# Whole last batch with eight PSUM banks in turn, and the first four weight pieces passed in halves (one core)

## The reference, cut to what matters

```
cond = einsum(x, W) + b + 2 * (x @ lora_As[slot]) @ lora_Bs[slot]      # x: (8, 512, 2048)
logits = einsum(cond, route_w)                                          # 8 experts
wh = one_hot(argmax(logits)) * max(logits) * einsum(cond, A)            # rank 16 each
out = x + einsum(wh, Bw)                                                # back to 2048
```

## Time and profile before

| | us |
|---|---|
| median of 3 runs | 286.09 (285.75 to 286.72) |
| profiled execution | 285.52 |
| its span | 283.7 |
| TensorE busy | 278.7 (98%) |
| VectorE busy | 201.8 (71%) |
| ScalarE busy | 112.5 (40%) |

### The profile page before, as it was taken

The page is one execution under the profiler, slowest core; times in us unless marked ns, Lnnn a source line. Parts: engine busy times, 40 slices in busy tenths (PEclk is TensorE's granted clock), DMA queues, the critical chain, the costliest instruction groups (busy, mean ns, idle before and its releaser), DMA issues.

```text
span 283.7 us, 4398 instructions
## 1 busy us (share of the span) xinstructions
PE 278.7 (98%) x1699; PEld 225.3 (79%) x1699; DVE 201.8 (71%) x234; ACT 112.5 (40%) x166; POOL 15.0 (5%) x46
## 2 busy tenths in 40 slices
PE   8999999999999999999999999999999999999994
PEld 5999999997766885888588758857885887588994
DVE  0052200077598999699789969996998798699975
ACT  0001301196786532734274355427432742442300
POOL 7600030000000000000000000000000000000000
PEclk9999999999999999999999999999999999999999
DMA  7999999999991066849967993999399769636668
GB/s 241 404 407 395 399 413 412 373 398 417 418 419 70 39 259 234 358 151 405 400 231 258 425 386 136 373 393 395 137 379 409 267 211 398 281 148 249 267 237 285
DMA packets 19303, 88.52 MB, mean 312 GB/s; under 512 B 2378, under 2 KB 4818, under 8 KB 11474
## 3 DMA queue, kind: packets, MB, share of 16 engines
q1 hardware_dynamic: 16128, 85.15, 76.8%
q10 hardware_dynamic: 3154, 3.09, 3.3%
HBM read 54.60 MB, written 33.55 MB: 311 GB/s over the span
## 4 chain that ended last, share of the span: by engine, by line
PE 98%; DVE 0%; DVEq 0%; issue 0%
PE bank_out L693 16%; PE bank_h L770 11%; PE bank_h L771 10%; PE bank_h L772 10%; PE bank_out L730 10%; PE bank_out L732 10%; PE bank_out L731 10%; PE bank_e L755 10%; PE bank_e L693 1%; PE bank_l L706 1%; PE bank_l L693 1%; PE bank_h L693 1%; PE bank_r L693 1%; PE bank_h L699 1%; PE bank_r L790 1%; PE bank_h L783 1%
## 5 line engine op out<-in xcount | busy, mean ns | idle before, releaser
L433 ACT ACTIVATE x_hi<-x_ring 128x1024 fp32r<-128x1024 f32 (+1 forms) x72 | 68.9, 965 | 63.5 <-PE bank_h L772 63.0
L535 DVE TENSOR_TENSOR x_lo<-x_ring,x_hi 128x1024 fp32r<-128x1024 f32 (+1 forms) x72 | 78.8, 1103 | 9.3 <-ACT x_hi L433 8.7
L628 DVE TENSOR_TENSOR x_ring<-bank_out,x_ring 128x1024 f32<-128x1024 f32 (+1 forms) x71 | 78.5, 1107 | 1.7 <-PE bank_out L732 1.3
L770 PE MATMUL bank_h<-x_hi,m_hi 128*128 128x512 f32 (+1 forms) x144 | 53.5, 372 | 0.0
L771 PE MATMUL bank_h<-x_lo,m_hi 128*128 128x512 f32 (+1 forms) x144 | 52.7, 366 | 0.0
L772 PE MATMUL bank_h<-x_hi,m_lo 128*128 128x512 f32 (+1 forms) x144 | 52.6, 366 | 0.0
L730 PE MATMUL bank_out<-wh_hi,bw_hi 128*128 128x512 f32 (+1 forms) x143 | 52.5, 367 | 0.0
L731 PE MATMUL bank_out<-wh_lo,bw_hi 128*128 128x512 f32 (+1 forms) x143 | 52.4, 366 | 0.0
L732 PE MATMUL bank_out<-wh_hi,bw_lo 128*128 128x512 f32 (+1 forms) x143 | 52.4, 366 | 0.0
L770 PEld LDWEIGHTS bank_h<-x_hi,m_hi 128*128 128x128 f32 x144 | 27.1, 188 | 11.2 <-issue 5.9
L693 PE MATMUL bank_out<-pt,w_ring 128*128 128x136 f32 x288 | 34.5, 279 | 0.0
(11 more groups left out here) (96 smaller groups left out, 188.7 us busy)
## 6 DMA issues: line engine op xcount, KB each, us to landing
x_ring<-xT SPq DMA_DIRECT2D x32, 1024.0 KB, 7.8
outT<-x_ring SPq DMA_DIRECT2D x28, 1024.0 KB, 5.0
w_ring<-W SPq DMA_DIRECT2D x30, 512.0 KB, 10.8
outT<-x_ring SPq DMA_DIRECT2D x12, 256.0 KB, 2.7
x_ring<-loraB ACTq DMA_DIRECT2D x8, 128.0 KB, 10.2
la<-loraA ACTq DMA_DIRECT2D x8, 128.0 KB, 13.1
x_ring<-BwT SPq DMA_DIRECT2D x1, 1024.0 KB, 11.6
pt<-PT SPq DMA_DIRECT2D x3, 272.0 KB, 8.9
```

Source lines behind the costliest of these rows:

```text
L433: act.activation(out, in_, ACT.Copy).then_inc(done, 1)
L535: dve.tensor_tensor(out, a, b, ALU.subtract).then_inc(done, 1)
L628: dve.tensor_tensor(x, out_banks(u, j), x, ALU.add).then_inc(v_out, 1)
L770: mm(h, m_hi[:, c, :], hi, start=(c == 0), stop=False)
```

## The change

Two edits. At the start, the first four pieces of W are all cut in two halves of two row chunks each, and TensorE passes over the four pieces twice: the first halves of pieces 0 to 3, then the second halves. At the end, the last batch is one unit of 512 tokens as the others are. Its output steps use all eight banks in turn, as four buffers of two (`bank_e` and `bank_h` become the two halves of `bank_eh`, `bank_r` and `bank_l` those of `bank_rl`), three output steps of batch 6 are held back behind its main product, and its stores are 512 KB per pair of chunks and 256 KB for each of the last two chunks. x and the output of the last batch lie in HBM as those of the other batches do. The diff, cut to its core:

```diff
-        UNITS = [(b, 0, T) for b in range(NB - 1)] + [(NB - 1, t, T // 2) for t in (0, T // 2)]
-        HELD = [2] * (NU - 1) + [3]
+        HELD = [2] * (NB - 1) + [3]
...
+        def w_bank(blk):
+            return (*bank_out, bank_eh, bank_rl)[blk] if blk < OPEN else bank_out[blk % 2]
+        def out_bank(b, j):
+            if b < NB - 1:
+                return bank_out[j % 2]
+            return (bank_eh, *bank_out, bank_rl)[j % 4]
+        def store_last(eng, c0, c1):
+            j = c0 // 2
+            k = NPIECES - NQ + 2 * T * j // PIECE
+            at = T * c0 % PIECE
+            eng.wait_ge(v_out, NP2 * (NB - 1) + (j + 1 if c1 - c0 == 2 else c1 - j))
+            eng.dma_start(outT[k, :, at:at + (c1 - c0) * T], x_ring[:, k % XRING, at:at + (c1 - c0) * T]).then_inc(d_last, 16)
...
+            def load_open(h):
+                sp.dma_start(head_sb[:, h, :], head[h]).then_inc(d_head[h], 16)
+                for n in range(1, OPEN):
+                    blk, part = ORDER[n]
+                    o = slice(h * HO, (h + 1) * HO)
+                    sp.dma_start(w_ring[:, n, o, :], W[blk, part, :, o, :]).then_inc(d_w_half[n - 1] if h == 0 else d_w[n], 16)
...
-            for n in range(NWP):
-                load_w(n)
+            for h in range(NHEAD):
+                load_open(h)
+            for n in range(OPEN - 1, NWP):
+                if n >= OPEN:
+                    load_w(n)
...
-            for u in range(NB - 1, NU):
-                for j in range(NP2):
-                    if u < NU - 1 or j % 2 == 0:
-                        store_pair(sp, u, j)
-            store_single(sp, 1)
+            for j in range(0, NP2 - 1, 2):
+                store_last(sp, 2 * j, 2 * j + 2)
+            store_last(sp, C - 1, C)
...
+            def w_open(h):
+                for n in range(OPEN):
+                    if n == 0:
+                        pe.wait_ge(d_head[h], 16)
+                    elif h == 0:
+                        pe.wait_ge(d_w_half[n - 1], 16)
+                    else:
+                        pe.wait_ge(d_w[n], 16)
+                    last = w_rows(n, h * HO, (h + 1) * HO)
+                    if h == NHEAD - 1:
+                        last.then_inc(t_w, 1)
...
+            for h in range(NHEAD):
+                w_open(h)
+            for n in range(OPEN, BP_AT):
                 w_piece(n)
...
+                if b == 0 and j < 2:
+                    pe.wait_ge(v_m, NWB)
+                elif b < NB - 1:
+                    pe.wait_ge(v_out, NP2 * b + j - 1)
+                elif j == 0:
+                    pe.wait_ge(v_two, NB)
+                    pe.wait_ge(v_wh, NB)
+                elif j == 3:
+                    pe.wait_ge(v_w, NB)
+                    pe.wait_ge(v_ahead, NB)
                 else:
+                    pe.wait_ge(v_out, NP2 * b + j - (2 if j < 3 else 3))
```

More of the change, by code:

```diff
@@ L215, in loads_in_slot, with x_pair @@
             return n // WRING + (1 if n % WRING else 0)
[L217 to L223, removed]
         def x_landed(eng, k):
             eng.wait_ge(d_x[k % XRING], 16 * (k // XRING + 1))
[L229 to L251, removed]
+        def x_pair(b, j):
+            at = 2 * T * j % PIECE
+            return x_ring[:, (NQ * b + 2 * T * j // PIECE) % XRING, at:at + 2 * T].rearrange("p (c t) -> p c t", c=2)
         WARM_UP = 8
@@ L437, in m_block, with split_hi @@
                 act.wait_ge(t_w, DONE[n])
[L438 to L447, removed]
+                sums = w_bank(n)[:, :, 0:PN]
+                copy(m_hi[:, 2 * n:2 * n + 2, :], sums[:, :, E:PN], a_m)
+                for i in range(2):
+                    copy(ext[i][:, 2 * n:2 * n + 2, 0:E], sums[:, :, 0:E], a_m)
+            def split_hi(b, j):
+                g = NP2 * b + j
+                if b == 0 and j < SRING:
                     act.wait_ge(t_w, NWP - WRING + j + 1)
@@ L648, in _ @@
                     if j < SRING:
-                        if j >= 2 or not short(u):
-                            split_lo(u, SRING + j)
-                    elif u + 1 < NU:
-                        split_lo(u + 1, j - SRING)
-                    if u >= 1 and 1 <= j <= NP2 - HELD[u]:
-                        add_x(u - 1, j - 1)
-                if u >= 1:
-                    weigh(u)
-                    add_x(u - 1, NP2 - HELD[u])
-                weigh_lo(u)
-                if u >= 1:
-                    for j in range(NP2 - HELD[u] + 1, NP2):
-                        add_x(u - 1, j)
+                        split_lo(b, SRING + j)
+                    elif b + 1 < NB:
+                        split_lo(b + 1, j - SRING)
@@ L662, in _ @@
+                    if b >= 1 and 1 <= j <= NP2 - HELD[b]:
+                        add_x(b - 1, j - 1)
+                if b >= 1:
+                    weigh(b)
+                    add_x(b - 1, NP2 - HELD[b])
+                weigh_lo(b)
+                if b >= 1:
+                    for j in range(NP2 - HELD[b] + 1, NP2):
+                        add_x(b - 1, j)
             for j in range(NP2 - 1):
-                add_x(NU - 1, j)
+                add_x(NB - 1, j)
             for i in range(2):
-                x = x_pair(NU - 1, NP2 - 1)[:, i, :]
@@ L671, in _, with w_rows @@
             mm = pe.matmul
+            def w_rows(n, o0, o1):
+                blk, part = ORDER[n]
+                for i in range(2):
+                    bank = w_bank(blk)[:, i, 0:PN]
+                    for o in range(o0, o1):
+                        k = part * WO + o
+                        for p in range(NPT):
+                            if blk == 0 and i == 0 and k == PT_PARTS[p][0]:
+                                pe.wait_ge(d_pt[p], 16)
+                        last = mm(bank, w_chunk(n, o, i), pt_chunk(k), start=(k == 0), stop=(k == C - 1))
+                return last
+            def w_open(h):
[9 more added lines that the diff above has]
+                        last.then_inc(t_w, 1)
             def w_piece(n):
```

288 lines of the change are left out of this document (102 added, 186 removed).

## The result

| | us |
|---|---|
| before, median of 7 runs | 286.09 (285.49 to 286.77) |
| changed, median of 7 runs | 287.63 (287.18 to 288.02) |
| ratio | 1.0051, interval [1.0034, 1.0067] |
| changed, profiled execution | 287.64, span 285.8 |

The change makes the kernel slower, by 1.54 us. The forecast was 286.8; the time is 0.83 above it (0.3%) and lies in the range, but the loss is about twice the 0.7 us that was forecast.

What follows compares the result with a forecast made beforehand. The prediction took the last store bytes, behind full DMA engines, to end the kernel, not the last matmul. Opening +0.25 and stores +0.5 us on 286.09 gave 286.8 us, range 285.7 to 288.3.

Steps and rivals of the forecast that it cites:

- The last bytes end both kernels: End: the last store bytes, at about 282.4 us before and 282.9 changed, set the end, not the last matmul.
- TensorE 1.36 earlier: End: with the last batch whole, the last matmul starts at 278.09 us against 279.45, 1.36 us earlier.
- no wait for `wh_lo`: Batch 7's first output step: three held steps cover the operand, ready about 0.8 us early; otherwise 0.6 us waited.
- Stores +0.5: End: stores with 4 KB rows at 403 GB/s end at 282.9 us against 282.4; bounds 0.1 to 1.8 us.
- The opening +0.25: Opening: TensorE's early gain is lost and it is 0.25 us late at piece 28 of W; range -0.15 to +0.9.
- the rows' cost of 0.4 us: Opening: four DMAs with 2 KB rows in place of 4 KB delay the full DMA stream by 0.4 us.
- W28 lands at a fixed time: Phase 1: the full DMA stream lands piece 28 of W at 60.48 + 0.4 us, however early it is issued.
- rival 4: Opening: its gain comes through, -0.5 us, with +0.5 at the end: 286.1, no change; chance 0.22 shared with another rival.
- Rival 1: End: 4 KB row stores leave at 440 GB/s or more, so the end follows VectorE: 285.1 us; chance 0.09.
- Rival 3: Both ends: W halves at 283 GB/s, pairs at 354, +0.9 and +1.8 us: 288.8; chance 0.14 with its like.
- What was to be seen: Changed profile: slow 4 to 9 us windows, last matmul near 278.3, full DMA share 270 to 283, last store over 3 us.
- The wait at W28: Phase 1: the first weight load of W's piece 28 waits for its DMA near 60.7 to 61.2 us.

Runs made afterwards that it cites:

- e1: The changed kernel with the opening of the kernel before, so only the whole last batch is changed: 287.50 us, ratio 1.0049 to the kernel before.
- e4: The changed kernel without ScalarE's stores of steps 1, 3 and 5 of the last batch (1.57 MB not written): 285.72 us, ratio 0.9985.
- e6: The changed kernel with two output steps held back at the last batch in place of three: 287.71 us, ratio 1.0056.
- e7: The changed kernel with the last batch's output through the two old buffers in turn, not four: 286.63 us, ratio 1.0030.
- e9: The changed kernel less two needless TensorE waits before the last batch's first output step, one instruction less: 287.05 us, ratio 1.0039.
- e5: The changed kernel with 192 more instructions (fulfilled waits) on TensorE's queue: 286.44 us, ratio 1.0015.
- e10: The kernel before with 64 more TensorE instructions, fulfilled waits ahead of the first 8 `bank_e` matmuls of each batch: 287.07 us, ratio 1.0031.
- e2: The kernel before with only the new opening, the first four pieces of W passed in halves: 285.66 us, ratio 0.9984.
- e3: The changed kernel with 96 more instructions (fulfilled waits) on TensorE's queue: 286.62 us, ratio 1.0022.
- e8: The kernel before with the new opening and its last batch's stores joined in twos to 4 KB rows: 286.24 us, ratio 1.0013.

## Why the prediction was right or wrong

- **The last bytes end both kernels: right.** e1 carries the loss, e4 takes it away, e6 and e7 delay TensorE by 0.6 and 1.1 us and the median does not follow.
- **TensorE 1.36 earlier, no wait for `wh_lo` that counts: right.** The last matmul was foretold for 278.09 without the opening's shift; it starts at 278.82 with one of 0.63, and 0.1 of waits. VectorE: 279.6 foretold, 280.31 less 0.63 is 279.7.
- **Stores +0.5: right in mechanism and rate, but not the whole end.** 403 GB/s was taken for 4 KB rows, 398 to 401 measured in these windows and 404 in e9's. The bulk ends at about 283.4, and 282.9 was foretold before the opening's shift. Without the load the profiles say +0.4 to +0.8 (43.0 to 43.4 against 42.6) and the medians +0.5 to +1.1, within the bounds of 0.1 to 1.8.
- **The missing term: one load of instructions.** The chain "the bytes end, the kernel ends" took the sixteen engines as one. 16 KB on a single engine take about 1 us: in the changed kernel's window from 275 to 276 us they are 6.0% of sixteen engines, 0.96 us of one. A store alone fills all sixteen (share 1.01 from 256.5 to 259.0), so the last one lands with the engine that is behind. That engine ends 1.5 us behind the others, more than the load's own 0.96; where the rest comes from is not shown. The load is worth 1.0 us in the profiles. In medians it is 0.4 by the two increases over the kernel before (changed 1.54, e9 1.13), 0.8 against e5, and 1.15 in e10. The sum was 0.83 too low, and this is the term that it lacked. That it falls there is inferred from the program's length: it is shorter by 97 matmuls and as many weight loads (1602 against 1699), so the place in it at which the last of the 13 loads is due comes later in time. Before, it was 266.9, when the stores had slack. Nothing in the earlier trace rows shows it; only the packets by queue do.
- **The opening +0.25: wrong in sign, and its mechanism with it.** e2 gives -0.46, interval -0.86 to -0.09. Two steps failed: the rows' cost of 0.4 us, and that W28 lands at a fixed time however early TensorE is. With the halves it landed at 60.62 in the changed kernel, 60.55 in e2, 60.8 in e3, 60.1 in e4, e6 and e9, and 59.8 in e5, e7 and e8. With the old opening it was 60.48, and 60.2 in e1 and 60.6 in e10. So no delay by short rows can be seen in a spread of 1.0 us. The wait that e3 shows at 60.84 is one execution's. In e5's, where the full rate came early, piece 4 starts at 11.68, 0.55 us earlier than before. W28 has landed at 59.8, and TensorE takes it at 60.09, 0.56 earlier:

```profile
60.09 1.93 PEld L612 LDWEIGHTS bank_out<-head_sb,w_ring 128*128 128x128 f32 x16
```

The gain passed through, as rival 4 has it (-0.5 for the opening), and e2's median fits that. Why it does not in e2's own profiled execution (60.66, as before) stays open. So does why it does not appear with the new end (e1 287.50 and changed 287.63, of different rounds).
- **Luck in the number.** The opening was put 0.7 us too high by e2 (+0.25 against -0.46), and the end lacked a term of about 1.0. The two errors go against each other, and the forecast came within 0.3% with the opening's half of its mechanism wrong.
- **Rival 1 (stores keep up at 440): wrong**: from 275 to 280 us the stores of the changed end move 397 to 406 GB/s in every kernel that has them all. **Rival 3: wrong**, 401 is not 354, and W28 was not 0.9 late. The Trainium skill, DMA: Bandwidth & Descriptors, Specifications, with 512 B as the least transfer for line rate, agrees with W28's landings, which the 2 KB rows of the opening did not delay, and not with the stores: 354 GB/s with 2 KB rows, 401 with 4 KB, 419 with 8 KB. The size of one store grows with the row in all three, so these runs do not tell the two apart.
- **What was to be seen:** the windows from 4 to 9 us under 396 (266, 373), the last matmul near 278.3 plus the shift, and the last store over 3 us (5.0) came true, and the share from 270 to 283 nearly so (0.93 to 1.03). (The windows say little: from 6 to 9 us e1, with the old opening, moves 376 GB/s.) The wait at W28 is missing in the changed kernel's profile, which the prediction had named as a sign of being wrong. TensorE's late rise to the full rate hides it there, but the landings above say the same.

The best of these kernels is e2, the opening without the new end: 0.9984 of the kernel before.

## What to carry to other kernels

When a kernel ends in stores that fill the DMA engines, count engine by engine: a share of 0.06 behind the bulk is one engine that is late, and the list of packets by queue says what else was moved in that stretch. A kernel whose program grows or shrinks by a few instructions can move its instruction loads; before crediting or blaming an edit for a microsecond, see whether a load came to lie in such a stretch. And make work on the compute engines shorter at the end only if the stores, from their own backlog, can follow.

## What the runs showed of the hardware

- TensorE's program came in loads of 16 KB, 13 in the changed kernel beside its 1602 passes and as many weight loads. One instruction less (e9) moved the last load from 275.5 us to behind the kernel's end, at 286.3; 64 more (e10) added a 14th to the kernel before. Each kept one DMA engine busy for about 1 us. With full queues the last store landed about 1 us later, 5.0 us behind its issue in the changed kernel and 4.0 in e9; with half-empty ones (e4, share 0.45) nothing was late.
- TensorE's full rate was reached at different times of the opening: the first eight weight loads took 1.14 us before, 1.16 in e5, 1.40 in e3, 1.70 in e2, 2.05 in e9 and 2.12 in the changed kernel, behind the same warm-up and with a granted clock recorded as 1.00. What decides it these runs don't tell. The Trainium skill, TensorE: Matmul & The Clock Gate, Part 1, says that the number of matmuls at the low level at a kernel's start differs from run to run; these six executions agree with that.
